# Second MoE layer: adding expert rows straight into the output, with zero rows sent to absent tokens

## The reference

```python
x = x + attention(layernorm(x))
x = x + ffn(layernorm(x))
x = x + rwkv(layernorm(x))
x = x + ffn(layernorm(x))

def ffn(x):                                  # x: [2048, 512]
    scores = sigmoid(x @ gate_w)             # 32 experts in 4 groups, 2 groups kept
    selected_experts = top_k(masked_scores, 6)
    weights = scores[selected] / sum(scores[selected])
    d = silu(rows @ w_gate[e]) * (rows @ w_up[e]) @ w_down[e]   # rows: the tokens of expert e
    expert_out = sum over the 6 experts of weight * d
    shared = silu(x @ sw_gate) * (x @ sw_up) @ sw_down
    return expert_out + shared
```

## Time and profile before

| | |
|---|---|
| median of 3 runs | 3315.62 us (3313.79 to 3316.78) |
| profiled execution | 3323.83 us |
| its span, first to last instruction | 3322.0 us |
| mean granted TensorE clock | 0.961 |
| TensorE busy | 3098.6 us (93%) |
| VectorE busy | 2076.6 us (63%) |
| ScalarE busy | 1588.8 us (48%) |
| POOL busy | 876.9 us (26%) |
| HBM read, written | 281.68 MB, 104.63 MB |
| adds into acc_rows | 232, 1634 ns each on POOL |
| gathers in the expert stages | 232, 1028 ns each on POOL |

### The profile page before, as it was taken

One profiled execution on the slowest core, in us unless ns is written; L12 is line 12 of the kernel. 1 busy time (PEld: TensorE's weight loads), 2 busy tenths in 40 slices (PEclk: granted clock), 3 DMA queues, 4 the chain that ended last, 5 costly groups with the idle time before them and its releaser, 6 DMA issues. The chain is left out here.

```text
span 3322.0 us, 62744 instructions
## 1 busy us (share of the span) xinstructions
PE 3098.6 (93%) x15674; PEld 2433.5 (73%) x15677; DVE 2076.6 (63%) x3842; ACT 1588.8 (48%) x2093; POOL 876.9 (26%) x767
## 2 busy tenths in 40 slices
PE   7979999999899899999999968878998999999996
PEld 6845555555578799899899933335788999999995
DVE  4256666663686466565566649988655666666664
ACT  2224444444321366565566656634124566666663
POOL 0021000100011233333333314430122444343332
PEclk9969999999899999999999979988999999999998
DMA  5331111230311467666676540114016777777754
GB/s 171 121 77 40 40 39 39 44 98 1 125 29 53 130 167 175 163 163 172 169 180 167 110 130 0 51 56 173 26 48 176 185 177 175 178 171 176 172 135 112
DMA packets 141481, 383.44 MB, mean 115 GB/s; under 512 B 22144, under 2 KB 22912, under 8 KB 137728
## 3 DMA queue, kind: packets, MB, share of 16 engines
q1 hardware_dynamic: 87616, 252.92, 24.1%
q0 software_dynamic: 52608, 127.69, 20.2%
q10 hardware_dynamic: 1152, 1.57, 0.2%
HBM read 281.68 MB, written 104.63 MB: 116 GB/s over the span
## 5 line engine op out<-in xcount | busy, mean ns | idle before, releaser
L1736 DVE TENSOR_TENSOR first_lo<-first_raw,first_hi x232 | 562.8, 2426 | 138.3 <-ACT first_hi L1679 138.3
L1633 POOL DMA_INDIRECT acc_rows<-g_y,first_ids_out x232 | 379.2, 1634 | 913.0 <-ACT g_y L1690 655.9
L1679 ACT ACTIVATE first_hi<-first_raw x232 | 469.5, 2024 | 67.7 <-DMA first_raw<-in_expert_weights_dram 43.6
L565 ACT ACTIVATE b_probs<-b_p_cols 128x1024 f32<-128x1024 f32 (+1 forms) x320 | 269.2, 893 | 301.0 <-PE b_p_cols L697 300.1
L1729 DVE TENSOR_TENSOR g_hidden<-g_gate,g_p_up 128x352 f32<-128x352 f32 x232 | 121.0, 521 | 441.3 <-PE g_p_up L1796 440.7
L1794 PE MATMUL g_p_gate<-first_hi,g_rows_hi 128*128 x928 | 321.6, 347 | 6.6 <-DVE first_lo L1736 6.5
L596 DVE TENSOR_REDUCE b_part_max<-b_p_ring 128x1 f32<-128x512 f32 x384 | 246.4, 686 | 118.1 <-PE b_p_ring L682 116.2
L1690 ACT ACTIVATE g_y<-g_p_y,first_rows_in 128x512 f32<-128x512 f32 x232 | 159.4, 687 | 324.5 <-PE g_p_y L1812 324.5
L1795 PE MATMUL g_p_gate<-first_lo,g_rows_hi 128*128 x928 | 302.7, 326 | 0.0
L1796 PE MATMUL g_p_gate<-first_hi,g_rows_lo 128*128 x928 | 301.7, 325 | 0.0
L1794 PE MATMUL g_p_up<-first_hi,g_rows_hi 128*128 x928 | 298.9, 322 | 0.0
(11 more groups left out here) (324 smaller groups left out, 6460.7 us busy)
## 6 DMA issues: line engine op xcount, KB each, us to landing
first_raw<-in_expert_weights_dram SPq DMA_DIRECT2D x248, 544.0 KB
acc_rows<-f_acc SPq DMA_DIRECT2D x34, 256.0 KB, 2.0
qk_hi<-a_hi SPq DMA_DIRECT2D x32, 256.0 KB, 2.6
qk_lo<-a_lo SPq DMA_DIRECT2D x32, 256.0 KB, 2.9
xn_rows<-f_xn SPq DMA_DIRECT2D x8, 1024.0 KB, 9.6
b_q_stack<-qk_hi SPq DMA_DIRECT2D x28, 256.0 KB
b_k_stack<-qk_hi SPq DMA_DIRECT2D x28, 256.0 KB
first_raw<-in_expert_weights_dram SPq DMA_DIRECT2D x2, 2176.0 KB, 8.7
```

The lines of the kernel that those rows point to most:

```text
L565: act.activation(probs[:, q, :, 0:w], p_cols[:, m % NCOL, :, 0:w], ACT.Exp, scale=SCALE).then_inc(probs_ready, 1)
L1633: pool.indirect_dma_start(out=acc_rows, out_offset=bass.IndirectOffsetOnAxis(ap=ids_out[:, i:i + 1].bitcast(U32), axis=0), in_=y[:, n, :], ...
L1679: act.activation(hi[:, bass.ds(place, PIECE)], raw[:, bass.ds(source, PIECE)], ACT.Copy).then_inc(split_hi_ready, 1)
L1736: v.tensor_tensor(lo[:, bass.ds(place, PIECE)], raw[:, bass.ds(source, PIECE)], hi[:, bass.ds(place, PIECE)].bitcast(F32), ALU.subtract).t ...
```

## The change

Spare rows of a tile no longer point behind the tokens when the tile is added. In both layers the router works out, for each expert e and each partition p, a token with the number p modulo 128 that did not choose e (the largest of the up to 16), and, should all 16 of them have chosen it, one that some other partition has. For each tile a product of these with "which tiles belong to expert e" gives 128 tokens, and `token_ids` holds them where the table has a spare row. The gather still uses `row_ids`, so a spare row still computes zeros; the add now goes by `token_ids` and adds the zeros to a real token. The accumulator therefore needs only T rows: in the first layer it is `mixed_rows`, in the second the output itself. The stores of zeros into the accumulator's spare rows and the last copy are gone.

```diff
         self.row_ids = sb("row_ids", [P, COLUMNS], I32)
+        self.token_ids = sb("token_ids", [P, COLUMNS], I32)
...
+        count_bank = p_count[:].rearrange("p t e -> p (t e)")
...
                 sp.dma_start(xn_rows[T:ROWS, D:D + E], acc[:, 0, 0:E]).then_inc(spare_stored, 16)
-                sp.dma_start(acc_rows[T:ROWS, :], acc[:, 0, :]).then_inc(spare_stored, 16)
...
                             for t in range(NROWS):
                                 v.tensor_copy(first.ids_in[:, t:t + 1], disp.row_ids[:, t:t + 1]).then_inc(first_ids_ready, 1)
+                            v.wait_ge(fill_done, 1)
+                            chain.link(v.scalar_tensor_tensor(table[:, 1, :], table[:, 0, :], 0.0, count_bank[:, 0:TILES], ALU.is_equal, ALU.mult))
+                            chain.link(v.tensor_tensor(table[:, 1, :], table[:, 1, :], table[:, 0, :], ALU.add))
+                            chain.step(v.tensor_scalar(disp.token_ids[:, TILES:], spare1[:].to_broadcast([P, COLUMNS - TILES]), -(T + 1.0), None, ALU.add))
+                            chain.link(v.tensor_scalar(disp.token_ids[:, 0:TILES], table[:, 1, :], -1.0, 0.0, ALU.add, ALU.max))
                             for t in range(2):
-                                v.tensor_copy(first.ids_out[:, t:t + 1], disp.row_ids[:, t:t + 1]).then_inc(first_ids_ready, 1)
+                                v.tensor_copy(first.ids_out[:, t:t + 1], disp.token_ids[:, t:t + 1]).then_inc(first_ids_ready, 1)
+                        if (i, f) == (2, 2):
+                            chain.link(v.tensor_scalar(place[:].rearrange("p t e -> p (t e)"), taken_b[:], -1.0, 1.0, ALU.mult, ALU.add))
+                            chain.link(v.tensor_tensor(place[:], place[:], token1[:].unsqueeze(2).to_broadcast([P, NT, E]), ALU.mult))
+                            v.tensor_reduce(absent1[:], place[:].rearrange("p t e -> p e t"), AX.X, ALU.max).then_inc(absent_ready, 1)
+                            chain.step(v.tensor_copy(ended[0:E, 0, :], end[0:E, :]))
+                            chain.link(v.tensor_tensor(diagonal[0:E, 0, :], total[0:E, :], ident[0:E, 0:E], ALU.mult))
+                            chain.link(v.memset(ended[0:E, 0, E - 1:E], float(COLUMNS)))
+                            chain.link(v.tensor_tensor(diagonal[0:E, 1, :], ended[0:E, 0, :], ident[0:E, 0:E], ALU.mult))
+                            chain.link(v.tensor_reduce(tile_span[0:E, :], diagonal[0:E], AX.X, ALU.add))
+                            chain.link(v.tensor_scalar(tile_span[0:E, 0:1], tile_span[0:E, 0:1], 1.0 / P, None, ALU.mult))
+                        if (i, f) == (2, 5):
+                            v.wait_ge(absent_turned, 1)
+                            chain.link(v.tensor_reduce(absent_e[0:E, :], count_bank[0:E, 0:P], AX.X, ALU.max))
+                            chain.step(v.tensor_copy(absent_t[:], count_bank[0:E, 0:P]))
+                            chain.link(v.tensor_scalar(absent_n[:], count_bank[0:E, 0:P], 0.0, absent_e[0:E, :], ALU.is_equal, ALU.mult))
+                            chain.link(v.tensor_tensor(absent_t[:], absent_t[:], absent_n[:], ALU.add))
+                            chain.link(v.tensor_scalar(span_hot[0:E, :], iota_t[0:E, :], tile_span[0:E, 1:2], None, ALU.is_lt))
+                            v.scalar_tensor_tensor(span_hot[0:E, :], iota_t[0:E, :], tile_span[0:E, 0:1], span_hot[0:E, :], ALU.is_ge, ALU.mult).then_inc(span_hot_ready, 1)
...
                         tables(i, g)
+                        if (i, g) == (2, 6):
+                            pe.wait_ge(absent_ready, 1)
+                            pe.wait_ge(column_row_read, 5)
+                            pe.transpose(count_bank[0:E, 0:P], absent1[:], ident).then_inc(absent_turned, 1)
+                        if (i, g) == (3, 2):
+                            pe.wait_ge(span_hot_ready, 1)
+                            pe.matmul(count_bank[:, 0:TILES], absent_t[:], span_hot[0:E, :], start=True, stop=True).then_inc(fill_done, 1)
...
-                    v.tensor_copy(ids_out[:, o:o + 1], disp.row_ids[:, bass.ds(t, 1)]).then_inc(ids_out_ready, 1)
+                    v.tensor_copy(ids_out[:, o:o + 1], disp.token_ids[:, bass.ds(t, 1)]).then_inc(ids_out_ready, 1)
...
-            xn_rows, acc_rows = k.dram(f"xn_rows{n}", [ROWS, D + E]), k.dram(f"acc_rows{n}", [ROWS, D])
+            xn_rows = k.dram(f"xn_rows{n}", [ROWS, D + E])
...
-        first_rows = layer(1, attention, None)
+        mixed_rows = k.dram("mixed_rows", [T, D])
+        layer(1, attention, None, mixed_rows)
...
-        second_rows = layer(2, None, time_mixed)
-        out_stored = k.sem("out_stored")
-        with nc.Block() as block:
-            @block.sync
-            def _(sp):
-                sp.dma_start(out2, second_rows).then_inc(out_stored, 16)
-                sp.wait_ge(out_stored, 16)
+        layer(2, None, time_mixed, out2)
```

More of the change, by code:

```diff
@@ L966, in stage_router @@
         spare1 = sb("spare1", [P, 1])
+        absent1 = sb("absent1", [P, E])
+        diagonal = sb("diagonal", [P, 2, E])
+        tile_span = sb("tile_span", [P, 2])
+        absent_e = sb("absent_e", [P, 1])
+        absent_t = sb("absent_t", [E, P])
+        absent_n = sb("absent_n", [E, P])
+        span_hot = sb("span_hot", [P, TILES])
         ended = sb("ended", [P, 4, E])
@@ L1014, in stage_router @@
         gate_ready, h_ready, hidden_hi_ready, hidden_lo_ready = sem("gate_ready"), sem("h_ready"), sem("hidden_hi_ready"), sem("hidden_lo_ready")
+        absent_ready, absent_turned, span_hot_ready, fill_done = sem("absent_ready"), sem("absent_turned"), sem("span_hot_ready"), sem("fill_done")
         down_done, acc_ready, lo_order = sem("down_done"), sem("acc_ready"), sem("lo_order")
@@ L1073, in _ @@
                     sp.wait_ge(xn_reloaded[i], 16)
-                sp.wait_ge(spare_stored, 48)
+                sp.wait_ge(spare_stored, 32)
                 sp.wait_ge(weights_stored, 16)
@@ L1107, in _ @@
                     pool.wait_ge(xn_stored[i], 16 * 2)
-                pool.wait_ge(spare_stored, 48)
+                pool.wait_ge(spare_stored, 32)
                 pool.wait_ge(weights_stored, 16)
@@ L1213, in add_rows @@
                     if n < 2:
-                        v.wait_ge(spare_stored, 48)
+                        v.wait_ge(spare_stored, 32)
                     else:
@@ L2259, in build, with layer @@
         ident = ctx.enter_context(nc.sbuf_tensor("ident", [P, P], F32))[:]
-        def layer(n, fill, source):
-            xn_rows, acc_rows = k.dram(f"xn_rows{n}", [ROWS, D + E]), k.dram(f"acc_rows{n}", [ROWS, D])
+        def layer(n, fill, source, acc_rows):
+            xn_rows = k.dram(f"xn_rows{n}", [ROWS, D + E])
             with ExitStack() as s:
@@ L2274, in layer @@
                 k.end_stage()
-            return acc_rows[0:T, :]
         def attention(resid):
@@ L2286, in attention @@
                 k.end_stage()
-        first_rows = layer(1, attention, None)
+        mixed_rows = k.dram("mixed_rows", [T, D])
+        layer(1, attention, None, mixed_rows)
         time_mixed = k.dram("time_mixed", [T, D])
-        stage_rwkv(k, ident, first_rows, mixes, decay, first, w_kvr, w_rwkv_out, time_mixed)
+        stage_rwkv(k, ident, mixed_rows, mixes, decay, first, w_kvr, w_rwkv_out, time_mixed)
         k.end_stage()
-        second_rows = layer(2, None, time_mixed)
-        out_stored = k.sem("out_stored")
-        with nc.Block() as block:
-            @block.sync
-            def _(sp):
-                sp.dma_start(out2, second_rows).then_inc(out_stored, 16)
-                sp.wait_ge(out_stored, 16)
+        layer(2, None, time_mixed, out2)
 def kernel(**inputs):
```

## The result

| | before | with the change |
|---|---|---|
| runs compared on one chip | 13 | 13 |
| median, us | 3311.3 (3299.73 to 3325.52) | 3300.67 (3293.44 to 3313.26) |
| ratio, 95% interval | | 0.9973 [0.996, 0.9985] |
| profiled execution, us | 3323.83 | 3313.26 |
| its span, us | 3322.0 | 3311.5 |

The kernel is faster by 0.27%, which is 8.9 us with an interval of 5.0 to 13.2 us. (The medians differ by 10.6 us; the text goes by the ratio, which has the interval.) Forecast were 14.2 us. The size of the gain is what has to be explained.

What follows compares the result with a forecast made beforehand. TensorE was taken to set the pace, with the final copy wholly on the path: 15.6 - 0.8 (TensorE's additions) - 0.6 (stall) = 14.2 us less, taking the median from 3315.62 to 3301.4 us, range 3297.0 to 3308.0 us.

Steps and rivals of the forecast that it cites:

- The removal of the copy: End of the kernel: the copy of acc_rows into the output lies wholly on the path; removing it saves 15.6 us.
- The zero store at no cost: Router start, both layers: dropping the store of 128 zero rows into acc_rows was priced at nothing.
- TensorE's two additions: Router, each layer: one transpose and one 128x152 product in plain f32, 0.4 us a layer, 0.8 us for both.
- The stall by the first piece: Router block 2: nine VectorE instructions, 3.2 us, delay one-hot tiles; TensorE stalls 0.3 us a layer, 0.6 us for both.
- the added product taking the ports ahead of POOL: Router, shared VectorE/GpSimd ports: POOL would be late instead, the stall 0 and the sum 0.6 us better.
- The second and third piece: Router, VectorE: six instructions of 2.0 us and four of 1.3 us, standing where VectorE waits or idles; priced at nothing.
- A: Router: nine added VectorE instructions uncovered, 3.2 us paid each layer; 8.4 us less, 3307.2 us; chance 0.09.
- B: Expert stage: adds land later; landings 1.5 us longer would give 3359 us; chance 0.05.
- C: Kernel's end: tail does not shorten, through a wait the copy hid or shifted transfers; about 3315.6 us, chance 0.04.
- D: Routers: no stall, transpose and product at 0.3 us, slightly shorter router starts; 16 us less, 3299.6 us, chance 0.12.

Runs made afterwards that it cites:

- The copy alone: Kernel before with its last block, the copy to the output, left out and the output unwritten: 3292.45 us against 3309.22 us, ratio 0.9956.
- half loads: Four kernels whose weight loads move half their words from the third expert on: before 3305.54 us, change 3294.57 us, before without copy 3288.9 us.
- the run with the unused table: Kernel before plus all router additions, worked out but not used; row ids, 2176 rows, zero store and copy kept: 3313.15 us, ratio 1.0021.
- the change again: The changed kernel, unedited, compared once more with the kernel before on the same chip: 3299.22 us, ratio 0.9971.
- the cheaper router: Changed kernel with VectorE's nine added instructions moved, the absent-token product's operands in fp32r and new tensors allocated behind acc: 3299.81 us, ratio 0.9965 against the kernel before.
- the first piece moved: Changed kernel with VectorE's nine added instructions behind block 2's second row sum instead of behind the product of chunk 2: 3311.86 us in one run.
- the unused tensors: Kernel before with the new SBUF tensors allocated in the changed kernel's places, no instruction added: 3315.71 us in one run.

## Why the prediction was right, and where it was not

**The removal of the copy: right.** 15.6 us were forecast from the issue to the end of the span. The copy alone measures 14.6 us (9.3 to 19.9), and 16.6 us with half loads; in the trace of the change nothing stands in its place.

**The zero store at no cost: borne out.** In the run with the unused table, which keeps the store, the routers take 245.46 and 245.63 us; in the change again, which has no store, 245.47 and 245.63 us.

**TensorE's two additions: mis-sized.** The forecast took 0.4 us a layer, by the row of table products, and kept 0.3 to 1.3 us as bounds. It was 0.08 + 0.62 = 0.70 us. The nearest row by size was the wrong one to lean on: the operands of the table products are fp32r, and the new product is plain f32, which goes through as two instructions. The fp32r version of it in the cheaper router costs 3.67 - 3.24 = 0.43 us.

**The stall by the first piece: right in kind, too small.** The mechanism came as described: the piece of 3.2 us, POOL's collision moved to the earlier group, the last tiles late, the next group unharmed. The term was 0.3 us a layer; it measured 0.78 us in layer 1 and 0.49 us in layer 2. The piece's length is not to blame. The term counted only by how much the tile is late. Each product that has to wait costs the group 0.4 to 0.5 us, where the row shows 0.16 us, and in layer 1 two of them waited. Moving the piece removed it.
The Trainium skill ("SBUF — State Buffer", the part on engine ports) gives the shared lock to whichever instruction starts first. The case that the prediction draws from it, the added product taking the ports ahead of POOL, did not arise: the product ran at 2410.26 us, POOL's subtraction at 2413.53 us. At the collision itself VectorE's one-hot tile is recorded as starting first, at 2413.50 us, and yet it is the one that is held, 1.42 us. But VectorE's rows overlap: the row_hot ahead of that tile ends only at 2413.30 + 0.28 = 2413.58 us, so POOL may have taken the ports before the tile could. The recorded starts neither bear the rule out nor refute it.

**The second and third piece: right.** No wait of TensorE or POOL names them. In layer 1 with the first piece moved, block 2 takes 52.90 us (from its first up product to that of block 3) and block 3 40.55 us (to the first gather), against 52.82 and 39.92 us with the unused tensors. That is 0.08 us for the transpose and 0.63 us for the product, and nothing is left for the pieces.

**Missing from the sum: the placement.** A step of table products takes 3.240 us instead of 3.228 us, and by the run with unused tensors the new places cost 0.64 us of layer 1's router. No term stood for it.

Together the traces give the routers some 3.5 us more: in layer 1 245.32 us against 243.36 us, and in layer 2 1.5 us in its last two blocks, from block 2's first up product to the first gather (53.39 + 40.53 us against 52.69 + 39.75 us). What lies ahead of these in layer 2 varies: the four profiles with the routers of before have 243.32 to 245.32 us for the whole of it. The forecast had 1.4 us. With the right sizes the sum is 15.6 - 3.5 = 12.1 us. With half loads 11.0 us was measured. With full loads it was 8.9, 9.6 and 5.3 us in three comparisons, 7.9 us in the mean, with intervals of 4 to 5 us to each side. Whether the last 4 us with full loads are chance or a real loss, such as a different meeting of loads and adds, stays open. The profiles can't tell: an expert stage takes 809 to 824 us in the full-load profiles of the kernel before with and without its copy, 809 to 820 us in those of the change.

**The rivals.** A (the first piece uncovered, 3.2 us a layer) is closest in the size of its gain, 8.4 us, but falls as a mechanism: the stall is 0.5 to 0.8 us. B (adds land later) falls: the adds take 4.9 us to the landing. POOL's waits for landings are 146.6 us over both layers in this execution; the kernel before has 122.9 us, and 143.4 us without its copy. With half loads it is 101.4 us against 95.1 us, and the expert stages are as long as before, so the changed adds show no cost of their own. C (the tail doesn't shorten) falls by the first timeline. D (more than the sum) falls, since the additions cost more than its 0.6 us.

## What to carry to other kernels

A copy from DRAM to DRAM with nothing behind it is worth its issue to the end of the span, and a work-around that avoids it pays if it adds less than that to the engine that sets the pace. Price what is added there by the distance between repeated groups, not by the duration of a row or by the wait named beside it, and by a row of the same data type before one of the same size; and expect about a microsecond of drift in such a stage as soon as new tensors shift others (here it was a loss both times). When runs differ by more than the effect, look for what the spread is made of, take it out of both kernels, and compare these.

## What the runs showed of the hardware

- The spread of 14 us and more between executions comes from the traffic of the weight loads. Four loads of an expert took about 6.2 us each in a row in one place; halving every load left 1.5 us of ScalarE's waits for them out of 41 us and a spread of 4.4 us. Halving the loads also relieves other transfers, so ScalarE's waits are the visible part and not shown to be all of it.
- A stretch of 5 us in which TensorE was busy 0.56 us was followed by 5 us at a granted clock of 0.50.
- Where tensors lie in SBUF changes TensorE's pace for identical matmuls: 3.228 or 3.240 us for a group of the router. Down products took 390 or 396 ns, most likely for the same reason.
- A plain f32 product of 152 columns on 32 rows costs 0.62 us in the stream, the same in fp32r 0.43 us.
- A reduction over 512 elements took 1.09 us through a pattern that is not contiguous, 0.69 us through one that is the earlier trace rows; nothing else was tested as the reason.
